# Merged scans: four of ScalarE's side jobs each one scan later in its queue

## What is computed

```python
def ss2d(x, in_w, conv_w, conv_b, xproj_w, dt_w, dt_b, A_logs, Ds, ln_g, ln_b, out_w):
    B, H, W, _ = x.shape
    d, N, K, R = (D_INNER, N_STATE, K_DIRS, DT_RANK)      # 96, 8, 4, 6
    L = H * W
    xz = jnp.einsum('bhwc,ec->bhwe', x, in_w)
    xa, z = jnp.split(xz, 2, axis=-1)
    xc = silu(dwconv3x3(jnp.transpose(xa, (0, 3, 1, 2)), conv_w, conv_b))
    ...                                                   # xs: xc in four directions
    delta = jax.nn.softplus(dts + dt_b[None, :, :, None])
    dA = jnp.exp(delta[..., None] * A[None, :, :, None, :])
    dBu = delta[..., None] * jnp.transpose(Bs, (0, 1, 3, 2))[:, :, None] * xs[..., None]
    def step(h, inp):
        a, bu, c = inp
        h = a * h + bu
        return (h, jnp.einsum('bkdn,bkn->bkd', h, c))
    ...
    y = jnp.transpose(ys, (1, 2, 3, 0)) + Ds.reshape(K, d)[None, :, :, None] * xs
    ...                                                   # ysum: the four directions summed
    yo = layernorm(yo, ln_g, ln_b) * silu(z)
    return jnp.einsum('bhwd,cd->bhwc', yo, out_w)

x = ss2d(x, ..._a)
x = ss2d(x, ..._b)
```

## Time and profile before

| | |
|---|---|
| median of 3 runs | 7986.28 us |
| the runs | 7963.08, 7991.41, 7986.28 us |
| the profiled execution | 7985.33 us |
| its span, first to last instruction | 7983.4 us |
| busy over the span: VectorE, GpSimd, ScalarE, TensorE | 81%, 69%, 66%, 78% |
| the phase of the change | 3402 to 6576 us of the span |
| mean granted TensorE clock | 0.856 of full speed |

### The profile page before, as it was taken

How to read it: one execution, slowest core, us unless ns; L and a number is a source line. 1 busy time by engine, 2 the same in 40 slices (tenths; PEclk the granted TensorE clock), 3 DMA queues, 4 the chain that set the end, 5 groups by cost and what they waited for, 6 DMA issues and landing times. The chain is left out here.

```text
span 7983.4 us, 105067 instructions
## 1 busy us (share of the span) xinstructions
PE 6266.9 (78%) x18336; PEld 2181.2 (27%) x18336; DVE 6478.1 (81%) x7496; ACT 5242.1 (66%) x10803; POOL 5481.8 (69%) x4416
## 2 busy tenths in 40 slices
PE   6878887677887785478888888888888777888686
PEld 2222222122222221122222222222222113488242
DVE  6998999779999997289999999999999994533636
ACT  6777777567777774366777777777777763222646
POOL 5888888668888885078888888888888981000606
PEclk8888888788888887688999999888888888997888
DMA  3444444344444444277777777777777772246312
GB/s 90 105 95 96 102 107 98 77 93 106 106 98 96 105 107 112 88 185 175 178 180 180 181 180 183 178 180 177 178 178 178 183 169 83 83 157 191 87 48 73
DMA packets 580429, 1050.78 MB, mean 132 GB/s; under 512 B 101719, under 2 KB 136812, under 8 KB 575180
## 3 DMA queue, kind: packets, MB, share of 16 engines
q1 hardware_dynamic: 580140, 1047.89, 54.6%
HBM read 858.09 MB, written 189.54 MB: 131 GB/s over the span
## 5 line engine op out<-in xcount | busy, mean ns | idle before, releaser
L1579 POOL TENSOR_TENSOR scan_prod<-scan_hs,scan_BC_rep 128x512 f32<-128x512 f32 x1536 | 1939.9, 1271 | 442.7 <-DVE scan_hs L1503 437.3
L600 POOL TENSOR_TENSOR mamba_prod<-mamba_hs,mamba_BC_rep 128x512 f32<-128x512 f32 x1536 | 1930.0, 1268 | 387.4 <-DVE mamba_hs L552 359.1
L552 DVE TENSOR_TENSOR_SCAN mamba_hs<-mamba_dA,mamba_carry,mamba_dbx 128x512 f32<-128x512 f32 x1152 | 1463.8, 1271 | 0.0
L1128 PE MATMUL scan_u_rep<-scan_du,scan_sel 96*128 96x512 f32 x1536 | 969.7, 717 | 472.9 <-DVE scan_hs L1503 472.1
L491 ACT ACTIVATE mamba_dA<-mamba_delta_rep,mamba_a_neg 128x512 f32<-128x512 f32 x1536 | 1090.2, 711 | 133.5 <-DVE mamba_hs L552 132.1
L1353 ACT ACTIVATE scan_dA<-scan_delta_rep,scan_a_neg 128x512 f32<-128x512 f32 x1536 | 1092.1, 712 | 90.4 <-DVE scan_hs L1503 77.7
L1503 DVE TENSOR_TENSOR_SCAN scan_hs<-scan_dA,scan_carry,scan_u_rep 128x512 f32<-128x512 f32 x768 | 976.6, 1272 | 161.0 <-ACT scan_carry L1333 157.6
L539 DVE TENSOR_TENSOR mamba_dbx<-mamba_u_rep,mamba_BC_rep 128x512 f32<-128x512 f32 x1152 | 788.8, 685 | 317.8 <-PE mamba_u_rep L314 132.1
L1503 DVE TENSOR_TENSOR_SCAN scan_hs<-scan_dA,scan_carry,scan_dbx_even 128x512 f32<-128x512 f32 x768 | 976.2, 1271 | 34.2 <-ACT scan_carry L1333 31.5
L282 PE MATMUL mamba_pre<-mamba_h,mamba_w_conv 96*96 96x512 f32 x1024 | 588.6, 715 | 324.2 <-POOL mamba_tails L568 272.5
L1890 POOL TENSOR_TENSOR ffn_sq<-ffn_xm 96x512 f32<-96x512 f32 x64 | 66.2, 1035 | 1030.5 <-DVE ffn_xm L1858 1019.7
(11 more groups left out here) (283 smaller groups left out, 10783.0 us busy)
## 6 DMA issues: line engine op xcount, KB each, us to landing
scan_BC_rep<-proj_rows SPq DMA_DIRECT2D x1024, 256.0 KB, 6.4
scan_delta_rep<-proj_rows SPq DMA_DIRECT2D x1024, 192.0 KB, 3.5
mamba_BC_rep<-bc_units SPq DMA_DIRECT2D x256, 512.0 KB, 10.3
mamba_delta_rep<-delta_units SPq DMA_DIRECT2D x512, 192.0 KB, 3.6
proj_rows<-scan_dbc SPq DMA_DIRECT2D x256, 224.0 KB, 2.6
delta_units<-mamba_delta SPq DMA_DIRECT2D x128, 192.0 KB, 6.3
by_n<-fin_res SPq DMA_DIRECT2D x32, 768.0 KB, 3.2
fmid_src<-by_n SPq DMA_DIRECT2D x32, 768.0 KB, 5.1
```

The costliest lines, as they stand in the source:

```text
L552: nc.vector.tensor_tensor_scan(hs[:, s % RING_H], dA[:, s % RING_A], dbx_bank(s)[:], carry[:, bass.ds(at, 1)], op0=ALU.mult, op1=ALU.add). ...
L600: pool.tensor_tensor(prod[:, (G * u + s) % RING_P], hs[:, s % RING_H], BC_rep[:, u, QUADS + s % QUADS], ALU.mult).then_inc(s_prod, 1)
L1128: nc.tensor.matmul(u_rep[c][:], sel[:, c], du[:, k], start=True, stop=True).then_inc(s_rep_u, 1)
L1579: pool.tensor_tensor(prod[:, (G * k + s) % RING_P], hs[:, (G * k + s) % RING_H], BC_rep[:, k, 2 + s % 2], ALU.mult).then_inc(s_prod, 1)
```

## The change

In ScalarE's `body` the places of four side jobs are each raised by one scan: the Silus with their two table loads from behind scan 12 to behind 13, `start_y` from 14 to 15, `square` from 15 to 16, and the two halves of softplus from behind s = 3 and s = 4 to behind s = 4 and s = 5. `rsqrt`, `affine`, `evict_out` and `copy_z` stay at their scans, and no other engine's queue changes.

```diff
@@ -1358,17 +1358,17 @@
                             carry_state(GC + at - RING_A, carried_before)
                         if has_out and at == 1:
                             copy_z(f)
-                        if at == 12:
+                        if at == 13:
                             if has_conv:
                                 silu_conv(conv, n + CH, at_xc)
                             if has_out:
                                 silu_z(f)
                             nc.scalar.preload_act_table_set(EXP_LN)
-                        if has_conv and at == 14:
+                        if has_conv and at == 15:
                             if has_out:
                                 act.wait_ge(s_mean, f + 1)
                             start_y(conv, n + CH, at_xc)
-                        if has_out and at == 15:
+                        if has_out and at == 16:
                             square(f)
                         if has_out and at == 23:
                             evict_out(f, out)
@@ -1376,10 +1376,10 @@
                             rsqrt(f)
                         if has_out and at == 20:
                             affine(f, out)
-                        if s == 3 and ahead:
+                        if s == 4 and ahead:
                             softplus_begin(lay if k + PRE < D else nxt_lay, j + PRE, (k + PRE) % D)
                             copy_bc(j + PRE, (k + PRE) % D)
-                        if s == 4 and ahead:
+                        if s == 5 and ahead:
                             softplus_end(j + PRE)
```

## The result

The changed kernel takes 8015.27 us (median of 6 runs, 8011.94 to 8025.93), the kernel before 7979.39 us (6 runs, 7963.08 to 7991.41): a ratio of 1.0049, 95% interval 1.0037 to 1.006. It is about 36 us slower and inside the range of 7960 to 8036. The ratio stands just under the 0.5% that the prediction took as the bound of "the same", and its interval reaches past it.

A forecast was written before the change was run, and what follows sets the result against it. VectorE's work was taken as the floor, its idle time as what could be won. Terms of -12.4, +13, +6 and +8 us made +15 on the profiled 7985.33 us, so 8000 us, range 7960 to 8036.

The forecast's parts named there:

- By class the sum: Tiles 1-7 -12.4 us, 8-39 +13, 40-55 +6, 56-62 +8, together +15.
- bound of +38: Tiles 8 to 39: upper bound, 1.18 us lost each, if `evict_out` comes as before and scan 24's `dA` was already last.
- rival B: Tiles with an output: scan 24's `dA` behind `evict_out` and softplus, up to 1.18 us each; 8028 to 8038 us; chance 0.20.
- The Silus: VectorE's wait at scan 13 moves to 14, shrinking 1.78 us to about 1.2; gain stays in tiles 1 to 7.
- c: The time in each tile at which ScalarE loads the table after waiting for the convolution; later times are counted from it.
- `affine` and the gate: `affine` stays at c + 18.03, so scan 21 waits near 1 us; gate at c + 22.9; over half the gain lost.
- Softplus behind `evict_out`: End of tile: softplus's 1.18 us stand between `evict_out` and scan 24's `dA`; scan 24 at c + 26.94, 0.47 us later.
- From scan 24 to the next c nothing changes.: End of tile to the next table load: no change, so scan 24's 0.47 us delay is the whole tile's difference.
- Tiles 40 to 55: Layer 1, 16 tiles: scan 24 later against c, 0.4 us each, +6 us; bounds -10 and +19.
- Tiles 56 to 62: No convolution, `evict_out` already last: 1.18 us lost in each of 7 tiles, +8 us; bounds 0 and +8.
- The waits listed as the test: VectorE: waits gone at scan 13, 1.1-1.3 us at 14, near 1 at 21, 1-1.5 at 24; tiles 8-39 near 94 us.
- The rule on the clock: TensorE after scan 19: shorter waits would keep 2.4 GHz; tiles 40 to 55 then cost +4 us, not +6.

The follow-up runs named there:

- e3: Changed kernel with `evict_out` written behind the second half of softplus at scan 23, nothing else: 7949.81 us, ratio 0.9963 to the kernel before.
- e7: e3 with `affine` moved from behind scan 20 to behind scan 21: 7946.69 us, ratio 0.9957 to the kernel before.
- e2: Kernel before with only the two halves of softplus one scan later: 8054.04 us, ratio 1.0094 to the kernel before.
- e4: Changed kernel with TensorE's projection of direction 3, at scan 0, done twice: 7996.38 us, ratio 1.0017 to the kernel before.
- e5: Changed kernel with `evict_out` behind softplus at scan 23 and the projection of direction 3 done twice: 7941.21 us, ratio 0.995 to the kernel before.
- e8: Changed kernel with `evict_out` behind softplus, `affine` behind scan 21 and the projection of direction 3 done twice: 7922.77 us, ratio 0.9931 to the kernel before.

## Why the prediction was right, and where it was short

The forecast was 8000 us in a range of 7960 to 8036, the result 8015, and slower than before was the side of its sum. That the number lies so near is in part luck. By class the sum had -12.4, +13, +6 and +8 us, together +15; the profiles have -8.1, +45.8, +0.2 and +7.7, and -1.9 in tile 0, together +43.7. Tiles 8 to 39 lie outside their own bound of +38, and in the profiled execution the other phases, which the change does not touch, took 15.6 us less. (The range was also said to take in rival B to its end; that end is 8038, 2 us outside.) Point by point:

*The Silus.* Right as a mechanism: the wait left scan 13 and 1.04 us (tiles 8 to 10 and ten of the 16 of layer 1) to 1.44 us of it stand at scan 14 in nearly all tiles from 8 on; 1.1 to 1.3 were forecast. In tiles 1 to 7 the term was mis-sized: 1.15 us each instead of 1.78. Those tiles end at c + 23.65 instead of c + 25.56, so the shift was kept whole, but c itself moved from 23.34 to 24.12 us behind scan 0, with TensorE at the lower clock behind scan 25 in each of them. That this comes from the change is not shown: e3 takes 47.8 us there too, and e7, with the same instructions in these tiles, 46.5.

*`affine` and the gate.* Right: `affine` at c + 18.03 in both kernels, the wait at scan 21 is 1.12 us ("near 1 us"), and e7 shows that it lay off the path.

*Softplus behind `evict_out`.* Right, and it is the heart of the case: scan 24 at c + 26.94 was forecast, and tile 8 has 26.94, the steady tiles 27.07 to 27.2. e3 and e2 show it from both sides.

*"From scan 24 to the next c nothing changes."* This step failed. It cost 1.05 us per tile in tiles 8 to 39 (22.81 to 23.86 us), 33 of the 46 us lost there. I had followed the late scan 24 on VectorE, ScalarE and GpSimd and not on TensorE: its work at scan 0 stands behind scan 23 and `evict_out` and not behind scan 24, so it was done 0.80 us earlier than before, counted from c; that and the late scan 24 turned into idle time ahead of the work behind scan 25, and that into a lower clock. Rival B had the lower clock, but in the wrong place, at the end of the tile, where it would have made `evict_out` late; that its 8028 us are near the result is luck as well.

*The trace had already shown it.* In the kernel before, the tiles of layer 1 that follow a wait of 2.27 us at scan 24 (tile 44) have c at 24.46 us behind scan 0 and 0.85 us of wait at the addition to Y, where tile 45 has 23.12 and none. I had read the waits at scan 24 and not what followed them. Such a wait allows the lower clock and does not force it: in the changed kernel 2.1 to 2.3 us stand at scan 24 in all of layer 1, and ten of its 16 tiles have c at 23.0 us all the same.

*Tiles 40 to 55* cost 0.2 us in all instead of 6: scan 24 is later against c (27.92, before 27.71), but c comes 0.2 us earlier behind scan 0, since this layer had the lower clock there in part of its tiles before as well. *Tiles 56 to 62* cost 7.7 us, 8 were forecast.

*The waits listed as the test* came as told, but for their sum in tiles 8 to 39, which was to stay near 94 us and is 141; in tiles 1 to 7 the waits of the scans fell from 17.9 to 7.4 us, where about 6 was forecast.

The rule on the clock was weighed at the wrong wait. What the rows show is that TensorE, after 1.85 us of waiting, ran at the lower of its two levels (0.56 granted over 6.9 us) and after 0.44 us at the upper one (1.00). The Trainium skill ("TensorE: Matmul & The Clock Gate", What's actually happening) tells of an idle TensorE falling to 1.2 GHz; by that rule, the trace agrees here. The length of one wait does not decide it alone, as the earlier trace rows showed; in tile 43 of the changed kernel TensorE waits longer at the same place, and the pair still runs at the upper level:

```profile
5563.76 1.13 PE L1128 MATMUL scan_u_rep<-scan_du,scan_sel 96*128 96x512 f32 x2 [2.32 <-DVE scan_hs L1503]
```

Two things stay open. One is what beside a wait decides TensorE's clock. The other is why nine of the 32 tiles of layer 0 in e3, and nine in e4, have `evict_out` at c + 25.1 or later and nearly all others at c + 24.2 to 24.5; no run was spent on it.

## What to carry to other kernels

When side jobs in an in-order queue are shifted together, look for the job that is not shifted: here two cheap instructions went from ahead of a wait to behind it, and swapping them back took 65 us off, which turned a loss against the kernel before into a gain. A wait removed in one place pays only to the next job whose time counts from another engine, so count each later job from what truly releases it. And follow a delay on TensorE too: work it did early becomes idle time ahead of its next wait, and that can cost its clock and so the next part of the loop.

## What the runs showed of the hardware

Added matmuls made a kernel faster: doing a projection of 1.87 us twice per tile took the changed kernel from 8015 to 7996 us, and the stretch behind it ran at the upper clock (1.13 us instead of 2.08 for the same pair). In the kernel before, where TensorE idled 0.44 us there, the same filler gave 7993 against 7984 us, a ratio of 1.001 with 1 inside its interval.

The lower clock, once there, mostly stayed. Tiles 8 to 10 of the changed kernel took 50.0 to 50.4 us; from tile 11 to 30 every tile had the low clock behind scan 25 and took 50.9 to 51.3 us. TensorE waited 1.84 to 2.02 us ahead of that work in each of them.

The same instructions have two rhythms. Tiles 1 to 7 take 47.8 us in the changed kernel and e3, and 46.4 to 46.7 us in e4, e5, e7 and e8, though e7 has in these tiles the very instructions of e3. In tile 4 of e3 and of e7 TensorE waits equally long behind scan 25, and the same pair runs at either level:

```profile
3600.85 2.07 PE L1128 MATMUL scan_u_rep<-scan_du,scan_sel 96*128 96x512 f32 x2 [1.30 <-DVE scan_hs L1503]
```

```profile
3589.26 1.13 PE L1128 MATMUL scan_u_rep<-scan_du,scan_sel 96*128 96x512 f32 x2 [1.30 <-DVE scan_hs L1503]
```

So 1.3 us per tile can come or go between two kernels without an edit to those tiles; whoever compares kernels by such a stretch should look at the granted clock first.
